# Embedding, attention and routed feed-forward of one core: quarter-array products, a second table layout and gathers issued one by one

## The reference

```python
ids = clip(item_ids, 0, 25000)                    # (128, 128)
item, geo, visit = emb[ids], geo_table[ids], visit_table[ids]      # 64, 64, 24 features
cat = concat([gelu(item @ w_item + b), gelu(geo @ w_geo + b), gelu(visit @ w_visit + b)])
h = item + 0.1 * layer_norm(gelu(cat @ w_fuse + b_fuse)) * (item_ids != 0)
h = h + attention(layernorm(h))                   # 4 heads of 16, rows of 128 tokens
h = h + routed_ffn(layernorm(h))                  # 63 of 128 tokens of a row, picked by a linear score
```

## Time and profile before

| | us |
|---|---|
| median of 3 runs | 517.92 |
| the three runs | 513.45, 517.92, 518.04 |
| the profiled execution | 516.32 |
| its span in the trace | 514.2 |
| mean granted clock of TensorE | 0.949 of full speed |
| busy: TensorE, its weight loads | 456.4 (89%), 360.1 (70%) |
| busy: VectorE, ScalarE, GpSimd | 404.8 (79%), 373.9 (73%), 343.8 (67%) |

### The profile page before, as it was taken

The page is one execution under the profiler, slowest core; times in us unless marked ns, Lnnn a source line. Parts: engine busy times, 40 slices in busy tenths (PEclk is TensorE's granted clock), DMA queues, the critical chain, the costliest instruction groups (busy, mean ns, idle before and its releaser), DMA issues. The chain is left out here.

```text
span 514.2 us, 16259 instructions
## 1 busy us (share of the span) xinstructions
PE 456.4 (89%) x5658; PEld 360.1 (70%) x5658; DVE 404.8 (79%) x1656; ACT 373.9 (73%) x662; POOL 343.8 (67%) x412
## 2 busy tenths in 40 slices
PE   4777799999999999999999999999998999788750
PEld 2455677777777777877777778777776877566530
DVE  1466888888888888889888888888886888877397
ACT  1226688888888888888888888888886888665440
POOL 5756677677777777777777767776867777311782
PEclk9899999999999999999999999999998999987755
DMA  4111111211111111111111111111101011000146
GB/s 111 24 26 26 27 27 27 27 26 25 25 25 23 20 22 21 23 20 20 25 25 25 25 25 25 25 25 25 25 14 22 15 24 26 1 4 3 41 122 163
DMA packets 23732, 15.80 MB, mean 31 GB/s; under 512 B 18848, under 2 KB 21536, under 8 KB 23584
## 3 DMA queue, kind: packets, MB, share of 16 engines
q0 software_dynamic: 6144, 9.97, 13.7%
q1 hardware_dynamic: 17568, 5.58, 4.0%
HBM read 11.08 MB, written 4.19 MB: 30 GB/s over the span
## 5 line engine op out<-in xcount | busy, mean ns | idle before, releaser
L312 POOL DMA_INDIRECT G<-table,idx x128 | 126.2, 986 | 62.6 <-issue 54.1
L320 POOL TENSOR_TENSOR rs<-ve,minus_half 128x4 f32<-128x4 f32 x96 | 101.2, 1063 | 28.7 <-DVE ve L660 27.6
L763 DVE TENSOR_REDUCE neg_max<-psum 128x4 f32<-128x512 f32 x128 | 84.4, 680 | 0.9 <-PE psum L1117 0.6
L449 ACT ACTIVATE prob<-psum 128x512 f32<-128x512 f32 x128 | 66.1, 602 | 3.2 <-PE psum L1087 2.9
L1045 PE MATMUL psum<-wt,hid 128*128 128x64 f32 x512 | 66.7, 286 | 1.5 <-ACT hid L456 1.5
L1045 PEld LDWEIGHTS psum<-wt,hid 128*128 128x128 f32 x512 | 63.0, 201 | 2.5 <-ACT hid L456 2.2
L1087 PEld LDWEIGHTS psum<-q_s,k_s 32*128 32x128 f32 x1024 | 32.8, 189 | 20.9 <-DMA q_s<-max_t 11.2
L1087 PE MATMUL psum<-q_s,k_s 32*128 32x128 f32 x1024 | 38.2, 285 | 9.5 <-ACT q_s L523 6.3
L807 DVE TENSOR_SCALAR k_s<-psum,wt 128x512 f32<-128x512 f32 x32 | 24.0, 751 | 28.5 <-PE psum L1198 28.5
L456 ACT ACTIVATE hid<-psum,wt 128x512 f32<-128x512 f32 x64 | 40.5, 683 | 4.8 <-PE psum L1218 2.0
L449 ACT ACT_TABLE_LOAD x31 | 39.8, 1283 | 3.4 <-PE psum L1087 2.9
(11 more groups left out here) (118 smaller groups left out, 1076.7 us busy)
## 6 DMA issues: line engine op xcount, KB each, us to landing
out<-R SPq DMA_DIRECT2D x13, 256.0 KB, 2.6
G<-table,idx POOLq DMA_INDIRECT x128
wt<-packed SPq DMA_DIRECT2D x1, 1028.0 KB, 5.1
q_s<-max_t SPq DMA_DIRECT2D x32, 8.0 KB
out<-R SPq DMA_DIRECT2D x1, 512.0 KB, 3.9
out<-R SPq DMA_DIRECT2D x2, 128.0 KB, 2.9
ids_sb<-ids SPq DMA_DIRECT2D x1, 64.0 KB, 1.8
```

The source lines that it names most:

```text
L312: pool.indirect_dma_start(G[par][:, b, :], None, table, bass.IndirectOffsetOnAxis(ap=idx[par][:, b:b + 1], axis=0),).then_inc(gathered[par ...
L320: pool.tensor_tensor(rs[:, :], ve[:, :], minus_half[:, :], ALU.pow).then_inc(S[dst], 1)
L449: act.activation(prob[:, :, h, :], bank[h].rearrange("p (b q) -> p b q", b=GB), ACT.Exp, scale=SCALE).then_inc(S["prob_ready"], 1)
L763: dve.tensor_reduce(neg_max[:, GB * h:GB * h + GB], bank[h].rearrange("p (b k) -> p b k", b=GB), AX, ALU.max, negate=True).then_inc(S["max ...
```

## The change

It has four parts.

1. `item_geo` becomes four products of 64 x 64 weights on the four quarters of the array, 256 columns each, in banks 6 and 7; `cat` is read from both. So that all four quarters are used, a second table `turned` holds geo before item, and rows 2 and 3 of a group are gathered from it. `visit` moves from bank 7 to bank 4, and its wait for `y_ready` moves to `item_geo`; waits of `x2_t` and `x3_t` are renamed to match.
2. `fuse` keeps the visit part, and its two 128 x 128 products become two of 128 x 64 in two column tiles. `w_fe` and `w_fo` become one `w_f`.
3. GpSimd gathers group `i + 4` instead of `i + 3`, and the four gathers are issued between its other operations: one after `rs3`, one after `add_x3`, two after `rs1`. `rs1` moves behind `base`; `u` gets two buffers. VectorE copies the indices of `i + 4`.
4. At the start the constant memsets and the first two copies of visit features move from GpSimd to VectorE, and GpSimd issues the gathers of groups 0, 1 and 2 in a row around `base(0)`, and those of group 3 at the end of step -2.

```diff
-            def fetch(g, par):
+            def fetch(g, par, first=0, end=GB):
...
-                for b in range(GB):
+                for b in range(first, end):
                     pool.indirect_dma_start(
-                        G[par][:, b, :], None, table,
+                        G[par][:, b, :], None, turned if b >= 2 else table,
...
             def base(g, par):
-                wait(pool, "h1_ready", 1, g - 1, alone=True)
+                wait(pool, "h1_ready", 1, g - 2, alone=True)
+                wait(pool, "u_ready", 1, g - 1, alone=True)
...
             fetch(0, 0)
-            pool.memset(minus_half[:, :], -0.5)
...
-            visit(0, 0, 0)
+            fetch(1, 1)
             pool.wait_ge(consts_ready, 1)
+            pool.wait_ge(zeros_ready, 3)
+            pool.wait_ge(gathered[0], 64)
             base(0, 0)
+            fetch(2, 0)
...
             def step(i, odd, half):
-                a, d, nxt = i + 2, i - 2, i + 3
+                a, d, nxt, far = i + 2, i - 2, i + 3, i + 4
+                steady = on(far) and not filling(i)
                 if on(d):
                     rstd(ve3, rs3, "ve3_ready", "rs3_ready", d)
-                if on(nxt):
-                    fetch(nxt, 1 - odd)
-                if on(a):
-                    rstd(ve1, rs1, "ve1_ready", "rs1_ready", a)
-                if on(nxt):
-                    visit(nxt, 1 - odd, half + 1 + odd)
+                if steady:
+                    fetch(far, odd, 0, 1)
                 if on(d):
                     weighted(d)
                 if on(d):
                     add_x3(d)
-                if on(nxt):
+                if steady:
+                    fetch(far, odd, 1, 2)
+                if on(nxt) and not (filling(i) and i == -2):
+                    visit(nxt, 1 - odd, half + 1 + odd)
+                if on(nxt) and not filling(i):
                     base(nxt, 1 - odd)
                 if on(a):
+                    rstd(ve1, rs1, "ve1_ready", "rs1_ready", a)
+                if steady:
+                    fetch(far, odd, 2, 3)
+                if steady:
+                    fetch(far, odd, 3, 4)
+                if on(nxt) and filling(i):
+                    base(nxt, 1 - odd)
+                if on(a):
                     rstd(ve2, rs2, "ve2_ready", "rs2_ready", a)
+                if type(i) is int and i == -2:
+                    fetch(3, 1)
...
             def item_geo(a):
-                wait(pe, "gt_out", 1, a)
-                wait(pe, "h2_ready", 1, a - 4)
-                mm(bank[6][:, :], w["w_ig"], ig_in[:, :], start=True, stop=True
-                   ).then_inc(S["ig_ready"], 1)
+                wait(pe, "gt_out", 1, a, alone=True)
+                wait(pe, "h2_ready", 1, a - 4, alone=True)
+                wait(pe, "y_ready", 1, a - 5, alone=True)
+                for n in range(2):
+                    for r in range(2):
+                        rows = slice(r * D, r * D + D)
+                        m = (n + r) % 2
+                        last = mm(bank[6 + n][m * D:(m + 1) * D, 0:2 * P], w["w_ig"][rows, m * D:(m + 1) * D],
+                                  ig_in[rows, n * 2 * P:(n + 1) * 2 * P], start=True, stop=True,
+                                  tile_position=(r * D, m * D))
+                last.then_inc(S["ig_ready"], 1)
...
                 mm(bank[6][:, 0:2 * P], w["w_fv"], catv[:, :], start=True, stop=False)
-                for n, wf in enumerate(("w_fe", "w_fo")):
-                    last = mm(bank[6][:, 0:2 * P], w[wf],
+                for n in range(2):
+                    last = mm(bank[6][n * D:(n + 1) * D, 0:2 * P], w["w_f"],
                               cat[:, :].rearrange("p (r s q) -> p s r q", r=2, s=2)[:, n],
-                              start=False, stop=(n == 1))
+                              start=False, stop=True, tile_position=(0, n * D))
```

More of the change, by code:

```diff
@@ L76, with build @@
 PACKED = _at
-def build(nc, ids, table, packed, out):
+def build(nc, ids, table, turned, packed, out):
     with ExitStack() as ctx:
@@ L107, in build @@
         idx = [sb(f"idx{p}", [P, GB], I32) for p in range(2)]
-        G = [sb(f"G{p}", [P, GB, FEAT]) for p in range(2)]
+        G = [sb(f"G{p}", [P, GB + 1, FEAT]) for p in range(2)]
         gv = sb("gv", [P, GB, VD])
@@ L123, in build @@
         s1 = sb("s1", [P, GB, D])
-        u = sb("u", [P, GB, D])
-        u0 = sb("u0", [P, GB, D])
+        u = [sb(f"u{p}", [P, GB, D]) for p in range(2)]
+        u_base = sb("u_base", [P, GB, D])
         c2 = sb("c2", [P, GB, D])
@@ L239, in filling @@
             return type(i) is int and i < 0
+        def filling(i):
+            return type(i) is int and i < 0
         def ffn_bank(d):
@@ L304, in _ @@
         def _(pool):
-            def fetch(g, par):
[L307 to L310, removed]
-                for b in range(GB):
+            def fetch(g, par, first=0, end=GB):
+                if first == 0:
+                    wait(pool, "idx_ready", 1, g, alone=True)
+                    wait(pool, "gt_ready", 1, g - 2, alone=True)
+                    wait(pool, "gv_ready", 1, g - 2, alone=True)
+                    wait(pool, "u_ready", 1, g - 2, alone=True)
+                for b in range(first, end):
                     pool.indirect_dma_start(
-                        G[par][:, b, :], None, table,
+                        G[par][:, b, :], None, turned if b >= 2 else table,
                         bass.IndirectOffsetOnAxis(ap=idx[par][:, b:b + 1], axis=0),
@@ L398, in step @@
                     rstd(ve2, rs2, "ve2_ready", "rs2_ready", a)
-            pipeline(pool, step, ahead=3)
+                if type(i) is int and i == -2:
+                    fetch(3, 1)
+            pipeline(pool, step, ahead=4)
             rstd(ve3, rs3, "ve3_ready", "rs3_ready", NG - 4)
@@ L612, in _ @@
         def _(dve):
+            dve.memset(minus_half[:, :], -0.5)
+            dve.memset(neg_max[:, :], 0.0)
+            dve.memset(o[:, :, :], 0.0).then_inc(zeros_ready, 1)
+            dve.wait_ge(zeros_ready, 1)
+            dve.memset(o[:, :, D:D + 1], 1.0).then_inc(zeros_ready, 1)
+            for p in range(2):
+                dve.memset(V[p][:, :, :, HD + 1:VC], 0.0)
+                last = dve.memset(V[p][:, :, :, HD:HD + 1], 1.0)
+            last.then_inc(zeros_ready, 1)
             dve.wait_ge(ids_in, 16)
@@ L620, in _ @@
             dve.wait_ge(ids_ready, 2)
-            dve.tensor_copy(idx[0][:, :], of(idx_all, 0)).then_inc(S["idx_ready"], 1)
+            for p in range(2):
+                dve.tensor_copy(idx[p][:, :], of(idx_all, p)).then_inc(S["idx_ready"], 1)
             dve.memset(ones[:, :], 1.0)
@@ L639, in _ @@
             setup_steps = 4
+            for p in range(2):
+                dve.wait_ge(gathered[p], 64)
+                wait(dve, "vt_ready", 1, p - 1)
+                dve.tensor_copy(gv[:, :, :], G[p][:, 0:GB, 2 * D:FEAT]).then_inc(S["gv_ready"], 1)
             dve.wait_ge(consts_ready, 1)
@@ L905, in step @@
                 if on(a):
-                    rows(a)
+                    rows(a, odd)
                 if on(e):
@@ L931, in step @@
                     route(d)
-            pipeline(dve, step, ahead=3)
+            pipeline(dve, step, ahead=4)
             take_weights(0)
@@ L1159, in x2_t @@
                 wait(pe, "x2_ready", 1, b)
-                ends(pe, "gt_out", 1, b + 1)
+                ends(pe, "catv_ready", 1, b + 1)
                 for j in range(2):
@@ L1169, in x3_t @@
                 wait(pe, "x3_ready", 1, d)
[L1170 removed]
+                ends(pe, "cat_ready", 1, d + 4)
                 for j in range(2):
```

49 lines of the change are left out of this document (25 added, 24 removed).

## The result

The changed kernel took 522.55 us (median of 14 runs, 517.75 to 524.71), the kernel before 515.82 us (median of 14). The ratio is 1.0109, 95% interval 1.0079 to 1.0139: slower by 1.1%, where I had forecast 506.5 us and a gain. Run again on another chip it gave 1.0086 (1.0052 to 1.0120). The profiled execution took 523.57 us, its span is 521.8 us, and TensorE's mean granted clock was 0.939 (before 0.949).

The account below looks back on a forecast made before the run. The prediction took a ScalarE-TensorE loop of 13.61 us as the bound, with a GpSimd gather loop of 13.53 as tight. 516.3 - 9.5 (steps) + 0.5 (start) - 1 (stall) = 506.3, left at 506.5; range 499 to 518.

Parts of the forecast that it names:

- The main loop: Loop of waits between ScalarE and TensorE holding both changed products; 13.61 us in the step shown, forecast from 13.65 to 13.33.
- the loop through the gathers: GpSimd from gv through four gathers and their landing to the next gv; 13.53 us, so a faster TensorE alone gains little.
- The products: TensorE's item and geo product gains 0.26 us and its fused product 0.06 per step, 0.32 together.
- the rival in which they take turns: Quarter products sharing a bank run in three rounds on TensorE, 0.86 us more; step 14.2, time 530.5; chance 0.08.
- The bank moves: Item and geo product's new wait for Y, covered by 0.18 us, and the visit product in bank 4; both cost nothing.
- GpSimd's new order: GpSimd's list from copied indices to rs1's end takes 7.05 us, in time by 0.3; loop 13.3, bounds 13.05 to 13.9.
- The moved term: GpSimd's time from the copied indices to the end of rs1 at its new place, claimed as 7.05 us.
- GpSimd becomes the bound: Rival: each singly issued gather costs 0.3 us more, rm waits for rs1 every step; step 13.6 to 13.7, 515.5; chance 0.15.
- the plain count: Rival: TensorE's change of tile form costs nothing more, 0.86 us leaves a step's products; time 501.5; chance 0.15.
- The start: First steps: the first root comes 3 us late behind gathers, other waits go; loss 0.5 us, between gain 2 and loss 3.
- The stall: GpSimd's single 2.13 us gap between two gathers, half covered by gathering a step ahead; gain 1 us, its occurrence chance.

Follow-up runs that it names:

- the root first: Changed kernel with GpSimd taking rs1 ahead of base instead of behind it: 511.08 us, 0.9889; on another chip 531.99 us, 0.9303.
- the best kernel: Changed kernel with rs1 ahead of base and the gathers of groups 2 and 3 reordered at the start: 506.58 us, 0.9812; again 506.25 us, 0.9822.
- the indices early: Changed kernel with VectorE copying the indices of i + 4 ahead of the last maxima of the step before: 511.53 us, 0.9902.
- the first job: Follow-up runs on one chip where the kernel before took 573.33 us; rs1 ahead of base took 531.99 us, with Y also moved earlier 535.27 us.
- the fourth job: Three variants of rs1 ahead of base with the start reordered (Y and indices early, Y early, old fused product): 530.51, 532.36, 529.16 us; kernel before 563.32.

## Why the prediction was wrong

**What bounds the kernel before: right.** The main loop and the loop through the gathers are both there. Products alone gain 0.1 a step and leave gv waiting; with the old products, the new gathers and the root first the step is 13.66, the main loop. That parts 1 and 2 need part 3 was shown from both sides.

**The products: right in mechanism, and a little too low.** By the trace the item and geo product gives 0.27 (1.50 before, 0.59 and 0.64 after) and the fused one 0.19, less 0.05 by which x2t starts later behind L1206: 0.14. I had 0.26 and 0.06. The quarters do run side by side, two row tiles in one bank, so the rival in which they take turns is refuted: it would have made L1169 to L1178 1.46, and the rows say 0.59. The Trainium skill, page "TensorEngine Tiling (Array Packing)", section "Gotcha 1: PSUM Pressure", says that different row tiles cannot access the same bank at the same time; here they do, on different partitions of it, and the measurement decides.

**The bank moves: wrong, by 0.15 to 0.22, once the rest is mended.** I had put the wait for Y at nothing, covered by 0.18. That cover was counted in a step of 13.6. When the step shrinks, Y, which hangs on VectorE, doesn't come earlier (it ends 1.10 and 1.19 behind the scores with the root first, 0.92 before), and the product stands 1.25 and 1.32 behind the scores instead of 1.10. That is 0.19 in the mean, and 0.27 + 0.14 - 0.19 = 0.22 is what both products together brought (0.21), 0.27 - 0.19 = 0.08 what the quarters did. In the changed kernel the wait of 0.55 is longer but follows from rm's and isn't a cost of its own: with parts 3 and 4 alone, where this wait isn't there, the step is the same.

**GpSimd's new order: this step failed.** The forecast's words were "That is 7.05, so rs1 ends at 262.1", in time by 0.3, and a loop of 13.3. Measured from the indices to the end of rs1: 7.74, and 0.24 until rm starts. (My terms add up to 7.01.) Of the difference 0.60 are the first gather: I took "starts some 0.3 behind the indices" and 1.6 to its end from a single row, but it starts 1.18 and ends 2.20 behind them. That row is from a step written out ahead of the loop. There the gather starts 0.28 behind the indices in the changed kernel too; inside the loop it starts 1.11 to 1.18 behind them in every step of all 20 traces, that of the kernel before among them. The gather that belongs to the very copy of the indices from which I counted (ready at 255.06) says it:

```profile
256.24 1.07 POOL L312 DMA_INDIRECT G<-table,idx  x1 [0.93 <-issue]
```

Another 0.23 is rs1, for which I took half of a double root; at its new place it starts while t still runs, and takes 1.23. The second gather was 0.10 cheaper and hid part of it. The moved term has a size of 7.98 and not 7.05; VectorE's part of the loop, 5.94, was 0.3 shorter than the 6.24 of the kernel before and gave some of it back. With slack of only 0.3 the sign of the whole was decided there: 27 steps of 0.60 more than my 13.3 are 16 of the 17.3 us between forecast and profiled time. The upper bound that I gave this loop, 13.9, is what was measured, but by luck: it stood for three gathers of 0.3 more each, and the two others cost no more than I took (1.15 and 1.26 against 1.25).

The rival "GpSimd becomes the bound" was the right mechanism, with rm waiting in each step, at 13.6 to 13.7 instead of 13.9. I gave it 0.15 because I charged it with 0.3 for each gather, and argued that the 0.86 us ahead of a first gather were already in my 1.6. They weren't: they are the late start that the step in the loop has and rows 6 hasn't. (The time under the plain count adds up to 501.8, not 501.5; nothing hangs on it.)

**The start: too cheap.** The root's delay was foreseen (22.4, measured 21.92), but I set the loss at 0.5 on the ground that other waits go. The table shows 4.3 lost up to the 8th scores: 1.1 is there at the first scores (34.79 against 33.70), 3.6 come in the next three steps (43.1 against 39.5 us), and 0.4 comes back in the four after. Put right together with the root the start was worth 4.5 us, alone 1.5. The part in the three steps is irregular: the best kernel took 42.4 us for them in one run and 39.9 in the other. In the changed kernel TensorE's granted clock was at its lower level, 1.2 GHz, three times in the first 66 us, for 3.4, 6.8 and 3.4 us, and in the kernel before once, for 3.4 us.

**The stall: right.** The two steps around it took 15.09 + 15.33 = 30.42 us before, 3.1 more than two others, and 16.53 + 13.34 = 29.87 after, 2.1 more: a gain of 1.0, as forecast. Only that such a gap is chance was wrong: it stands ahead of the 114th gather of the program in all 20 traces, 2.13 us before and 1.33 instead of 0.16 in the changed kernel. Its cause stays open.

## What to carry to other kernels

A cover of a few tenths of a us is no cover: when an instruction that another engine waits for is moved behind others, add them up at their new neighbours' price, from rows in which the same pair of engines is busy and of the same part of the program (a step written out and one in a loop differed by 0.9 us here), and compare the slack with the error of that sum before the gain with anything. Put the one small operation that is waited for ahead of the bulk that nobody waits for; here this exchange of two calls turned 1.1% slower into 1.1% faster, and with the start in order 1.8%. A covered wait that is moved must be counted again in the shorter step.

## What the runs showed of the hardware

**A gather's start in a loop.** In the loop the first gather of a step started 1.11 to 1.18 us behind the copy of its indices in every run, whatever VectorE did then; in the steps written out ahead of the loop it started 0.28 behind it, where it waited for nothing else. In the changed kernel this puts it 0.12 or 0.17 behind the end of x, which looks like a wait for x but isn't one: with the indices early it keeps its distance from them and starts beside x. What the 0.9 us in the loop are stays open.

**GpSimd and VectorE.** The operation t took 0.80 instead of 0.42 where it started while u ran, and ended 0.30 behind it. The root took 1.23 instead of 1.04 where t was still running at its start. The Trainium skill, page "SBUF — State Buffer", section "SBUF: two separate sides", says that a VectorE operation with two SBUF inputs and a GpSimd operation that reads SBUF exclude each other for a whole instruction. Between t and u the trace agrees; between t and the root it agrees only where t comes first, for with the root first t ran its 0.42 within the root. A gather's issue beside the same two operations x took 1.64 to 1.71 us in one run, 1.02 to 1.04 in another and both in turn in a third, so x beside it can't be all of the reason.

**Two kinds of chips.** The kernel with the root first ran on both: 532 us and steps of 14.3 on the first, 511 us and 13.45 on the second. On the first, the maxima wait for the scores though nothing else is different. VectorE, then GpSimd, of that run:

```profile
249.73 1.29 DVE L799 TENSOR_REDUCE neg_max<-psum 128x4 f32<-128x512 f32 x2 [0.72 <-PE psum L1155]
```

```profile
248.06 0.95 POOL L328 DMA_INDIRECT G<-turned,idx  x1 [0.30 <-issue]
```

The scores started at 247.57, so their results are seen 2.16 us later, 0.72 behind the end of the gather (249.01); on the other chip there is no such wait. The same offset to a gather's end, 0.70 to 0.74, is there in each of 20 steps of both kernels of the first job with the root first, and one of 0.61 to 0.72 in the three of the fourth job. What causes it stays open. Its consequence is that the order of the variants depends on the chip: on the first, the change's place for rs1 with the old products came out at 0.9108, and root first, the better order elsewhere, at 0.9303. These two differ in the products too, so that the place of the gathers against the scores is the reason is argued, not shown.
